# Cross-attention: the softmax shift written by 32-row matmuls ahead of the product passes of two tiles

## The reference

```
q = (x @ w_q)            # 16 heads of 64, 512 queries in each of 4 batches
k, v = context @ w_kv    # 1601 keys in each batch, width 256 before the projection
attn = softmax(q @ k^T * 64 ** -0.5)
out = (attn @ v) @ w_out + b_out
```

## Time and profile before

| | before |
|---|---|
| median of three runs | 2050.33 us |
| the profiled execution | 2053.94 us |
| its span, first to last instruction | 2052.2 us |
| cross-attention, approximately | 230 to 1760 us of the span |
| TensorE busy | 1746.8 us (85% of the span) |
| VectorE, ScalarE, GpSimd busy | 1191.0, 832.0, 1323.0 us |
| mean granted TensorE clock | 0.919 of 2.4 GHz |

### The profile page before, as it was taken

The page is one execution under the profiler, slowest core; times in us unless marked ns, Lnnn a source line. Parts: engine busy times, 40 slices in busy tenths (PEclk is TensorE's granted clock), DMA queues, the critical chain, the costliest instruction groups (busy, mean ns, idle before and its releaser), DMA issues. The chain is left out here.

```text
span 2052.2 us, 32755 instructions
## 1 busy us (share of the span) xinstructions
PE 1746.8 (85%) x10682; PEld 1212.3 (59%) x10682; DVE 1191.0 (58%) x2046; ACT 832.0 (41%) x1228; POOL 1323.0 (64%) x711
## 2 busy tenths in 40 slices
PE   7553599999989999998999999899999998509990
PEld 5443466666656666665666666566666664408980
DVE  4788555556565656556565665655565654553345
ACT  3111234444444444444444444444444444224440
POOL 2988338577676667576776676675766677454544
PEclk8775689999999999999999999999999999559995
DMA  5000200000200000010000001000000000321223
GB/s 185 1 21 24 79 1 22 1 22 0 73 1 22 22 3 22 0 52 22 21 1 23 1 21 52 21 22 1 21 1 21 15 1 1 124 84 63 71 63 128
DMA packets 37813, 68.09 MB, mean 33 GB/s; under 512 B 3560, under 2 KB 27504, under 8 KB 36656
## 3 DMA queue, kind: packets, MB, share of 16 engines
q1 hardware_dynamic: 33936, 56.12, 8.1%
q0 software_dynamic: 3744, 10.23, 1.5%
HBM read 52.84 MB, written 13.50 MB: 32 GB/s over the span
## 5 line engine op out<-in xcount | busy, mean ns | idle before, releaser
L1001 POOL TENSOR_TENSOR xa_total<-xa_total,xa_pexp 128x1024 f32<-128x1024 f32 (+1 forms) x352 | 852.9, 2423 | 52.7 <-ACT xa_pexp L942 27.3
L1060 DVE TENSOR_REDUCE xa_parts<-ps_ring 128x1 f32<-128x402 f32 x1024 | 532.3, 565 | 299.8 <-PE ps_ring L887 292.8
L942 ACT ACTIVATE xa_pexp<-ps_s 128x1024 f32<-128x1024 f32 (+1 forms) x416 | 422.7, 1025 | 419.0 <-PE ps_s L842 391.9
L856 PE MATMUL ps_pv<-xa_pexp,xa_v 128*64 128x512 f32 (+1 forms) x1664 | 399.8, 604 | 0.0
L887 PE MATMUL ps_ring<-xa_k_hi,xa_q_hi 64*128 64x402 f32 x1024 | 235.0, 377 | 32.7 <-DVE xa_parts L1060 31.4
L856 PEld LDWEIGHTS ps_pv<-xa_pexp,xa_v 128*64 128x64 f32 (+1 forms) x1664 | 106.2, 137 | 181.9 <-issue 148.3
L887 PEld LDWEIGHTS ps_ring<-xa_k_hi,xa_q_hi 64*128 64x128 f32 x1024 | 142.7, 186 | 118.2 <-DVE xa_parts L1060 58.9
L1001 POOL TENSOR_TENSOR xa_total<-xa_pexp 128x1024 f32<-128x1024 f32 x32 | 76.3, 2384 | 190.9 <-ACT xa_pexp L942 189.6
L1048 DVE TENSOR_TENSOR xa_k_lo<-ps_ring,xa_k_hi 128x402 fp32r<-128x402 f32 (+1 forms) x128 | 73.6, 575 | 214.7 <-ACT xa_k_hi L953 214.7
L842 PE MATMUL ps_s<-xa_q_hi,xa_k_hi 64*128 64x512 f32 (+1 forms) x832 | 194.0, 433 | 3.6 <-DVE xa_k_lo L1048 2.8
L842 PE MATMUL ps_s<-xa_q_neg,xa_row_one 64*128 64x512 f32 (+1 forms) x832 | 174.4, 393 | 0.0
(11 more groups left out here) (263 smaller groups left out, 2946.2 us busy)
## 6 DMA issues: line engine op xcount, KB each, us to landing
wa_raw<-in_pack_a SPq DMA_DIRECT2D x17, 768.0 KB, 4.4
ex_w_raw<-in_pack_e SPq DMA_DIRECT2D x8, 1026.0 KB, 5.3
ctx_raw<-in_ctxT SPq DMA_DIRECT2D x4, 1601.0 KB, 8.5
wb_raw<-in_pack_b SPq DMA_DIRECT2D x16, 256.0 KB, 2.6
ex_w_hi<-ybuf SPq DMA_DIRECT2D x8, 512.0 KB, 7.6
sa_xT<-in_xT SPq DMA_DIRECT2D x8, 256.0 KB, 6.4
X<-in_x SPq DMA_DIRECT2D x1, 2048.0 KB, 11.5
x_hi<-sa_x1s_hi SPq DMA_DIRECT2D x16, 128.0 KB, 2.1
```

The lines of the kernel that those rows point to most:

```text
L856: ins = nc.tensor.matmul(ps_pv[half(h), :], v[0:m, t, at:at + XD], pexp[0:m, buf, h, :], start=t == 0, stop=t == MT - 1)
L942: nc.scalar.activation(pexp[0:m, buf], ps_s[0:m, (p * MT + t) % 2], ACT.Exp, scale=XD ** -0.5)\
L1001: nc.gpsimd.tensor_tensor(total[p][0:m], first, pexp[0:m, buf], ALU.add).then_inc(s["add_done"], 1)
L1060: nc.vector.tensor_reduce(parts[:, h, q, c:c + 1], ps_ring[:, r, 0:CW], AX.X, ALU.max)\
```

## The change

The fourth pass leaves S. A new step SX stands in front of S at every even tile and writes the shift into both score buffers, for tile t and tile t + 1, with one pass of four matmuls: (t, head 0) on rows 0 to 31 of the array, (t, head 1) on 32 to 63, (t + 1, head 0) on 64 to 95 and (t + 1, head 1) on 96 to 127. At t = 12 it has two matmuls. They start the accumulation, and the three product passes of S are added to it. SX waits until the exponential of tile t - 1 is done, where S waited only for that of tile t - 2. Ones and maxima now stand in rows 0, 32, 64 and 96, for which `negmax` is reduced with twice the output, in two instructions as before.

```diff
@@ block
         some(MX_BEFORE[t])
+        if t % 2 == 0:
+            steps.append(("SX", p, t))
         steps.append(("S", p, t))
@@ cross_attention
+        def buf_of(p, t):
+            return (p * MT + t) % 2
+
+        def shifted_with(t):
+            return (t,) if t == MT - 1 else (t, t + 1)
@@ tensor, handle
                 if kind == "S":
                     p, t = st[1:]
+                    m, ms = rows(t), slice(t * P, t * P + rows(t))
+                    for q, (kk, qq) in enumerate(((k_hi[p][:, ms], q_hi[p]), (k_lo[p][:, ms], q_hi[p]),
+                                                  (k_hi[p][:, ms], q_lo[p]))):
+                        for h in range(2):
+                            ins = nc.tensor.matmul(ps_s[0:m, buf_of(p, t), h, :], kk[half(h)], qq[half(h), :],
+                                                   start=False, stop=q == 2)
+                    ins.then_inc(s["scores_ready"], 1)
+                elif kind == "SX":
+                    p, t = st[1:]
                     if t == 0:
                         r, c = n.job(("SH", p))
                         pe.wait_ge(drained[r], c)
-                    need(pe, s["exp_done"], n.of("S") - 1)
-                    m, ms = rows(t), slice(t * P, t * P + rows(t))
-                    for q, (kk, qq) in enumerate(((k_hi[p][:, ms], q_hi[p]), (k_lo[p][:, ms], q_hi[p]),
-                                                  (k_hi[p][:, ms], q_lo[p]), (row_one[:, 0:m], q_neg[p]))):
-                        for h in range(2):
-                            ins = nc.tensor.matmul(ps_s[0:m, t_of(n), h, :], kk[half(h)], qq[half(h), :],
-                                                   start=q == 0, stop=q == 3)
-                    ins.then_inc(s["scores_ready"], 1)
+                    both = shifted_with(t)
+                    need(pe, s["exp_done"], n.of("S") - 2 + len(both))
+                    for g, (u, h) in enumerate((u, h) for u in both for h in range(2)):
+                        at, m = slice(32 * g, 32 * g + 32), rows(u)
+                        nc.tensor.matmul(ps_s[0:m, buf_of(p, u), h, :], row_one[at, 0:m], q_neg[p][at, :],
+                                         start=True, stop=False)
@@ vector
-            for h in range(2):
-                nc.vector.memset(att[h * XD:h * XD + 1, 0:P], 1.0).then_inc(s["zero_set"], 1)
-            dve.wait_ge(s["zero_set"], 3)
+            for g in range(4):
+                nc.vector.memset(att[32 * g:32 * g + 1, 0:P], 1.0).then_inc(s["zero_set"], 1)
+            dve.wait_ge(s["zero_set"], 5)
@@ vector, SH
-                    for h, col in ((0, 0), (1, XD)):
-                        nc.vector.tensor_reduce(negmax[:, :, col:col + 1], parts[:, h], AX.X, ALU.max, negate=True)\
+                    for h in range(2):
+                        nc.vector.tensor_reduce(negmax[:, :, 32 * h::XD].rearrange("p q g -> p g q"),
+                                                parts[:, h].unsqueeze(1).broadcast_to([P, 2, NC, 4]), AX.X, ALU.max, negate=True)\
                             .then_inc(s["shift_ready"], 1)
```

## The result

The changed kernel takes 2094.44 us (median of four runs, 2092.89 to 2097.01), the one before 2050.67 in the same comparison. It is slower by 43.8 us; the ratio is 1.0213, with a 95% interval of 1.020 to 1.0225. The forecast was 2097, within 2060 to 2122. The profiled execution took 2094.69 us, its span is 2093.0.

A forecast was written before the change was run, and what follows sets the result against it. TensorE's stream was taken to bound the kernel: 65.2 us of grouping changes, less 3.1 under cover and 15.4 of real gains, gave +46.7 on the profiled 2053.9, 2100.6; 2097 us as median of runs, range 2060 to 2122.

The forecast's parts named there:

- Price of a change of grouping: On TensorE around SX: each change costs 0.205 us, emptying 0.095 plus uncovered load 0.11; 318 changes, 65.2 us.
- free: Rival: changes between 64 and 32 rows around SX cost nothing, -15.4 to -44.4 us, 2035 to 2006; chance 0.15.
- half price: Rival: at changes around SX only the emptying is paid, the load hides; +14.8 us, 2065; chance 0.11.
- One pass for four matmuls: In SX: four matmuls side by side cost one pass, 0.231 us; 192 passes removed, 44.4 us.
- the matmuls two by two: Rival: SX's four matmuls run two by two, 0.23 us more for each SX, 2141 us; chance 0.05.
- the load in two turns: Rival: only SX's weight load takes two turns, 0.11 x 224 = 24.6 us, 2122; no separate chance given.
- MX to SX: Sign in the timeline after: from MX to SX 0.28 us instead of 0.19.
- t = 1: At tile 1, K follows and nothing waits, so the removed pass is saved fully: 31 x 0.231 = 7.2 us.
- t = 3 and t = 7: At tiles 3 and 7, waits for ring slots VectorE must reduce swallow the removed pass: saving 0.
- t = 5: At tile 5, the second MX waits for its ring slot; 0.13 of 0.231 stays, 31 x 0.13 = 4.0 us.
- t = 9, p = 1: At tile 9 of blocks with p = 1, the removed pass keeps a saving of 0.8 us in all.
- The added wait at t = 12, p = 0: SX(12) waits for tile 11's exponential; the saving of t = 11 is gone, 0 beyond.

The follow-up runs named there:

- experiment 3: The kernel before, with the fourth pass of S on 32-row pieces, so two changes of grouping a tile: 2173.98 us, ratio 1.0599.
- experiment 1: The changed kernel with SX on 64 rows, four matmuls in two passes, no added change of grouping: 2073.23 us, ratio 1.0117 to the kernel before.
- experiment 8: The changed kernel with MX reduces over 101 of the 402 columns: 2024.93 us, ratio 0.9871 to the kernel before.
- experiment 6: The changed kernel with one MX pair of each block moved from in front of tile 7 to tile 6: 2072.51 us, ratio 1.0105 to the kernel before.
- experiment 4: The kernel before without any shift pass, exponentials at a scale of 0.001, computing another result: 2006.91 us, ratio 0.9784.
- experiment 5: The kernel before with one MX pair of each block moved from in front of tile 7 to tile 6: 1988.35 us, ratio 0.9684.
- experiment 12: The changed kernel with that MX pair moved to tile 6 and each GpSimd sum split into two halves: 2042.06 us, ratio 0.9958 to the kernel before.

## Why the prediction was right, and where it was off

The terms are checked by the distance of the starts of neighbouring S steps, after less before, median over 15 blocks of p = 1: from t = 0 to 1 -0.24 us, 1 to 2 +0.20, 2 to 3 -0.24, 3 to 4 +0.52, 4 to 5 -0.13, 5 to 6 +0.43, 6 to 7 -0.31, 7 to 8 +0.52, 8 to 9 -0.22, 9 to 10 +0.52, 10 to 11 -0.22, 11 to 12 +0.35, 12 to the next +0.25. Their sum is 1.43 us a block; 1.435 in the mean for p = 1 and 1.433 for p = 0, and 31 blocks of it are 44 us. The start of S is that of its load, which at t = 4 and 12 is uncovered only since the change; this shifts up to 0.11 us from one distance to the next. At t = 10 it was uncovered in the kernel before too, behind an MX pair that came late for its slot. There the first and the second pass are 0.33 apart:

```profile
909.30 0.59 PE L842 MATMUL ps_s<-xa_q_hi,xa_k_hi 64*128 64x512 f32 x2
909.63 0.49 PE L842 MATMUL ps_s<-xa_q_hi,xa_k_lo 64*128 64x512 f32 x2
```

- **Price of a change of grouping.** Predicted 0.205 between 64 and 32 rows, from rows of 128 and 64. Measured 0.095 and 0.11 again (904.26 to 904.70, 904.70 to 905.04), and 0.19 to 0.205 by experiment 3. The rivals "free" and "half price" fall. By the Trainium skill ("TensorEngine Tiling (Array Packing)", Key Properties) a change of mode drains the array, and this trace agrees; the uncovered load, 0.11 of the 0.205 us, comes on top of what that sentence says.
- **One pass for four matmuls.** Right: 0.44 from SX to S less 0.11 and 0.095 is 0.235 us, and experiment 3, with two matmuls of 32 rows in the pass, has 0.43 at the same place. The four loads take 0.19 us, as two do, so the rivals with the matmuls two by two or the load in two turns fall too. By the Trainium skill's page "TensorE: Matmul & The Clock Gate" (Part 3) four such tiles give 3.07 times the throughput. I had turned that into an estimate of 0.30 us a pass; this trace does not show such a surcharge.
- **MX to SX.** I said 0.28 us and it is 0.37 (903.89 to 904.26). No cost was missed: MX follows V there, so its own load of 0.11 is uncovered, in the kernel before too. The sum had it, the sentence on what would show it did not.
- **Where savings vanish.** t = 1: 0.20 added between tiles 1 and 2, as for a full saving. t = 3 and t = 7: lost, as said. t = 5: I kept 0.13 of 0.231; 5 to 6 shows +0.43 instead of 0.21, all of it lost. The term missed the load of a matmul that waits. The second MX at 906.38 comes late for its slot, and PV follows 0.50 us behind the pair where 0.28 was usual: 0.13 of wait, and some 0.1 of load that the wait uncovers. t = 9, p = 1: I kept 0.05. Tiles 9 to 11 together took 0.29 us more, where two changes are 0.41 with the saving all lost and 0.18 with all of it kept; that the load of S at t = 10 was uncovered already, as shown above, can account for it. At p = 0, tiles 6 to 10 together took 0.26 us more, against 0.50 at p = 1: the added change at t = 8 does lie under the wait for `att`.
- **The added wait at t = 12, p = 0.** It is there: in 13 blocks the load of SX starts some 0.03 us behind the end of that exponential. But it costs nothing, since MX to SX is 0.37 us as at p = 1. I let it eat the saving of t = 11; tiles 10 to 12 took 0.13 us longer in the median at p = 0 and at p = 1, so about half of the saving came through, as I had it for p = 1. In the mean of p = 0 it is 0.32. That comes from two blocks, 2.3 and 1.0 us longer, in which the granted clock was 0.63 (592.3 to 599.2 us) and 0.67 (1364.5 to 1371.0) of 2.4 GHz in the trace after, so at its lower level of 1.2 for most of that time, against 1.00 and 0.79 in the same tiles before.
- **Tile 12.** Its 65 columns make the uncovered loads shorter: SX to S is 0.37 there and 0.44 elsewhere. That is about 0.12 us a block, 4 us, that I had charged too much.
- **The reduces to `negmax`.** I put them at nothing; they last 184 ns instead of 167, 1 us in all 64.

By these rows the misses are +4 us for t = 5 (more lost than said), about -4 for tile 12, -2 for t = 11 at p = 0, and -3 for tiles 6 to 11 (probably the cheaper change at t = 10, which was not tested apart). The two blocks at a low clock add some 3 us in the profiled execution. That the sum of +46.7 came within 3 us of the measured +43.8 is luck in part, because the misses nearly cancel. The mechanism is not: experiments 1, 3 and 8 show its two parts, the exchange of passes for changes at 21 to 23 us, and as much again that the ring takes. The effect of such changes can't be added up freely, though: experiment 6 was missed by 41 us between partners, because of where `att` fell against GpSimd's sums.

## What to carry to other kernels

Merging small matmuls onto finer row groups did not pay here, because their neighbours use another grouping: price the entry and the exit, an emptying and an uncovered load each, against the passes saved. Before counting a removed pass as time, follow what stands behind it to the next semaphore; a high busy share doesn't show this slack, and leaving the work out altogether is the cheap way to learn its worth. Where waits for a small ring of buffers recur at one place, move one job across the long step next to it; here one pair moved in a list brought 3.2%, more than the 2% of experiment 4.

## What the hardware showed beyond that

VectorE's product of two operands in SBUF (128x512, 0.69 us) and GpSimd's sum (128x1024, 2.38 us) did not run at once. In the kernels before, after and of experiments 5 and 6, every product (`att` or its low part) that began inside a sum, with 0.15 us or more of it left, ended 0.55 us behind the sum's end, with lengths of 0.81, 1.78 (the low part, of the same form), 2.28 and 2.67 us by how much of the sum was left, while a sum that began inside a product lasted 2.72 instead of 2.38 us. Reduces out of PSUM that ran wholly beside a sum kept their 0.57 us. The Trainium skill ("GPSIMD Engine Reference", 1. Specifications) says that GpSimd's SBUF interfaces are shared with VectorE, with contention for instructions with two SBUF inputs; this trace agrees. That the one who comes second waits for the end of the other's instruction is what the constant 0.55 us says here. That halving the sums was the cause of the full 30 us in experiment 12 is likely, but not separated from the shift of phase that it brings. The kernel of experiment 5 with halved sums wasn't run.
